# A CIN and DNN recommender kernel on one Trainium2 core: a rebuilt opening, in which TensorE turns the pair fields of the first two chunks

## The reference, cut to what matters

```
inputs = emb[feature_ids] * feature_vals[:, :, None]        # 1024 x 39 x 16
h = inputs
for i in range(3):                                          # sizes 200, 200, 200
    x = einsum('bhd,bmd->bhmd', h, inputs).reshape(B, -1, 16)
    x = relu(einsum('bcd,oc->bod', x, W[i]) + b[i])
    if i != 2: h, direct = x[:, :100], x[:, 100:]
    else: direct = x
    finals.append(direct)
d = relu(relu(inputs.reshape(B, -1) @ D0.T + d0) @ D1.T + d1)
out = concat(sum(finals over the 16), d) @ fc_W.T + fc_b + sum(bias_emb[ids] * vals)
```

## Time and profile before

| what | us |
|---|---|
| median of 3 runs | 2806.42 (2805.46 to 2812.66) |
| the profiled execution | 2815.94 |
| its span, first to last instruction | 2813.8 |
| PE busy in the span | 2652.6 (94%) |
| first matmul | 102.0 |
| PE without a gap from | 165.1 |

### The profile page before, as it was taken

The page is one execution under the profiler, slowest core; times in us unless marked ns, Lnnn a source line. Parts: engine busy times, 40 slices in busy tenths (PEclk is TensorE's granted clock), DMA queues, the critical chain, the costliest instruction groups (busy, mean ns, idle before and its releaser), DMA issues.

```text
span 2813.8 us, 66205 instructions
## 1 busy us (share of the span) xinstructions
PE 2652.6 (94%) x17912; PEld 2642.9 (94%) x17912; DVE 2269.9 (81%) x4563; ACT 1825.8 (65%) x4774; POOL 2256.7 (80%) x1921
## 2 busy tenths in 40 slices
PE   0279999999999999999999999999999999999998
PEld 0179999999999999999999999999999999999987
DVE  1278888888888888888887888888888888888873
ACT  0266767667666666666666767676766666666653
POOL 5388888888888888888888888888888888877753
PEclk9989999999999999999999999999999999999998
DMA  9734464444545464544554455545554546454531
GB/s 178 171 81 129 122 162 122 125 125 123 160 112 138 113 170 115 137 115 132 152 132 116 119 150 135 133 119 134 150 134 116 136 119 163 114 135 113 136 106 28
DMA packets 204534, 363.66 MB, mean 129 GB/s; under 512 B 66097, under 2 KB 118988, under 8 KB 204236
## 3 DMA queue, kind: packets, MB, share of 16 engines
q1 hardware_dynamic: 174080, 344.02, 44.7%
q0 software_dynamic: 10656, 2.92, 3.3%
q10 hardware_dynamic: 19628, 15.27, 2.0%
HBM read 357.87 MB, written 26.75 MB: 137 GB/s over the span
## 4 chain that ended last, share of the span: by engine, by line
PE 92%; ACTq 2%; POOL 1%; issue 1%; DMA 1%; SPq 1%; DVE 1%; ACT 0%; POOLq 0%; DVEq 0%
PE acc L564 60%; PE acc L565 28%; PE acc L586 2%; PE hrep L597 1%; ACTq L703 1%; DMA lin<-w 1%; POOL raw L441 1%; ACTq L682 0%; POOL xlo_p L487 0%; POOL prod_p L481 0%; DMA xs<-xt 0%; PE hrep L653 0%; SPq L295 0%; PE acc L632 0%; PE acc L631 0%
## 5 line engine op out<-in xcount | busy, mean ns | idle before, releaser
L564 PE MATMUL acc<-W,xhi_d 128*128 128x400 f32 x5632 | 1733.8, 367 | 15.7 <-DVE xlo_d L943 15.6
L565 PE MATMUL acc<-W,xlo_d 128*128 128x200 f32 x5632 | 1435.9, 255 | 0.0
L943 DVE TENSOR_TENSOR xlo_d<-prod_d,xhi_d 128x512 fp32r<-128x512 f32 (+1 forms) x1536 | 983.1, 640 | 220.2 <-ACT xhi_d L741 215.3
L935 DVE TENSOR_TENSOR prod_d<-hrep,xrep 128x512 f32<-128x512 f32 (+1 forms) x1536 | 1039.0, 677 | 100.5 <-ACT hrep L777 34.9
L487 POOL TENSOR_TENSOR xlo_p<-prod_p,xhi_p 128x512 fp32r<-128x512 f32 (+1 forms) x768 | 959.2, 1249 | 176.8 <-ACT xhi_p L735 128.4
L565 PEld LDWEIGHTS acc<-W,xlo_d 128*128 128x128 f32 x5632 | 1079.6, 192 | 0.0
L564 PEld LDWEIGHTS acc<-W,xhi_d 128*128 128x128 f32 x5632 | 1061.1, 188 | 17.4 <-DVE xlo_d L943 17.1
L564 PE MATMUL acc<-W,xhi_p 128*128 128x400 f32 x2944 | 917.8, 363 | 133.7 <-POOL xlo_p L487 133.7
L741 ACT ACTIVATE xhi_d<-prod_d 128x512 fp32r<-128x512 f32 (+1 forms) x1536 | 887.0, 578 | 236.4 <-PE acc L565 220.6
L481 POOL TENSOR_TENSOR prod_p<-hrep_s,xrep 128x512 f32<-128x512 f32 x512 | 667.4, 1304 | 163.7 <-ACT hrep_s L772 113.4
L565 PE MATMUL acc<-W,xlo_p 128*128 128x200 f32 x2944 | 751.8, 255 | 0.0
(11 more groups left out here) (79 smaller groups left out, 913.8 us busy)
## 6 DMA issues: line engine op xcount, KB each, us to landing
xrep<-xs SPq DMA_DIRECT2D x384, 384.0 KB, 4.3
l0x<-xs SPq DMA_DIRECT2D x384, 136.5 KB
xrep<-xs SPq DMA_DIRECT2D x384, 128.0 KB, 4.7
xrep<-xs SPq DMA_DIRECT2D x128, 336.0 KB, 5.1
xrep<-xe SPq DMA_DIRECT2D x128, 96.0 KB, 5.5
xe<-xs SPq DMA_DIRECT2D x40, 256.0 KB, 3.6
l0x<-xs SPq DMA_DIRECT2D x384, 19.5 KB
lin<-w ACTq DMA_DIRECT2D x8, 750.0 KB, 7.8
```

Source lines behind the costliest of these rows:

```text
L564: pe.matmul(bank[:, 0:2 * OUTS], hi, w, start=first, stop=last, skip_group_check=True)
L565: return pe.matmul(bank[:, 0:OUTS], lo, w[:, 0:OUTS], start=False, stop=last, skip_group_check=True)
L935: nc.vector.tensor_tensor(to, h, xrep[:, (par + layer - 1) % 2, a:a + count, :], ALU.mult).then_inc(s_prod_d, 1)
L943: op = nc.vector.tensor_tensor(xlo_d[:, slot, 0:split], bank[:, 0:split], xhi_d[:, slot, 0:split].bitcast(F32), ALU.subtract)
```

## The change

- Table rows: the ids of tile 0 alone are worked out first, straight into `idx`, so that the gathers wait neither for the values nor for a copy on POOL.
- W1: its rows and its load are issued by SP (at the start) and no longer by ACT; ACT issues W0's 9 DMAs, splits W0 and all of W1, and then issues W2's rows. SP issues the load of W2 after the blocks of chunk 1. Both loads have 13 DMAs where they had 17.
- DVE splits W0 and W1, and only then scales tile 0 (`first_scale`; POOL did it).
- Layer 0 of chunks 0 and 1 needs no DRAM: DVE lays the pair fields out by samples in `xrep` (`lay_out_pairs`), PE turns them (`first_inputs`, 8 transposes for a chunk), DVE copies them to `l0x` (`first_layer0`).
- DVE turns the first `EARLY` = 4 chunks by themselves, and SP stores those ahead; the 12 others are turned later and stored after W2's load.
- W2 is split inside step 1, a piece each after D3, D4, D5 and D6; PE waits for the pieces one by one (`W2_NEEDED`).
- `xe` is gone. Block 3 is loaded out of `xs` by four DMAs where it had two.
- In the loop, store and `dense_in` come one chunk later, and the gathers are dealt out anew: 9 in step 0 and 6 in step 1 (12 and 9 before).

```diff
-            def split_weights(layer):
+            def split_weights(layer, n):
...
+            dve.wait_ge(s_ids_in, 16)
+            table_rows(slice(0, FIELDS), idx[:], 0)
+            table_rows(slice(0, TILES * FIELDS), idi[:], 4)
...
-            split_weights(0)
-            turn_inputs(0, False)
+            split_weights(0, [0])
+            split_weights(1, range(len(PIECES[1])))
+            first_scale()
+            dve.wait_ge(s_xin, 2)
+            lay_out_pairs(0)
+            turn(0, EARLY, s_xt0)
+            lay_out_pairs(1)
+            first_layer0(0, (prod_d[0], prod_d[1]))
+            turn(EARLY, DIM, s_xt)
+            first_layer0(1, (prod_d[2], acc[2]))
             dve.wait_ge(s_fc, 32)
             evacuate(0, 0)
-            split_weights(1)
...
-            split_weights(2)
...
+            def first_inputs(c, banks):
+
+                pe.wait_ge(s_pairs, 2 * c + 2)
+                for n in range(L0_SLOTS):
+                    t = pe.transpose(banks[n // 4][0:L0_ROWS, n % 4 * P:(n % 4 + 1) * P], pairs(c)[:, n, :], ident[:])
+                    if n % 4 == 3:
+                        t.then_inc(s_pt, 1)
...
-            store_inputs(0)
-            sp.wait_ge(s_xs, 128)
-            load_layer0(0)
+            sp.wait_ge(s_xt0, 1)
+            store_rows(0, 0, EARLY, s_x0)
+            sp.wait_ge(s_x0, 128)
             sp.wait_ge(s_wlo, W_DONE[0])
-            for e in (1, 2, 0):
+            for e in (1, 2, 0, 3):
                 load_block(0, 0, e)
-            spread_inputs(0)
-            sp.wait_ge(s_prod_p, p_num(-1, 1) + 1)
-            load_layer0(1)
-            sp.wait_ge(s_one, 16)
-            sp.wait_ge(s_xe, 16 * XE_DMAS)
-            load_block(0, 0, 3)
-            for e in (1, 2, 0, 3):
-                sp.wait_ge(s_xblk[e], 32)
-                load_block(1, 1, e)
+            sp.wait_ge(s_pt, 4)
             sp.wait_ge(s_prod_p, p_num(0, 1) + 1)
             load_layer0(2)
+            for e in (1, 2, 0, 3):
+                sp.wait_ge(s_xblk[e], BLOCK_SEM[e])
+                load_block(1, 1, e)
+            load_weights(sp, 2, w2)
+            sp.wait_ge(s_xt, 1)
+            store_rows(0, EARLY, DIM - EARLY, s_xs)
+            store_dense_inputs(0)
             step(1, 0)
```

More of the change, by code:

```diff
@@ L81, in step_order @@
 def step_order(i):
-    return [g for g in ORDER if layer_of(*g) in present(i)]
+    order = [g for g in ORDER if layer_of(*g) in present(i)]
+    if isinstance(i, int) and i == 0:
+        order.sort(key=lambda g: layer_of(*g))
+    return order
 def p_num(i, k):
@@ new lines, in rows_of_weights @@
+        def rows_of_weights(engine, layer, src):
+            used = H_QUARTER * FIELDS
+            full = used // QUARTER
+            for q in range(4):
+                rows = lin[layer][used * q:used * (q + 1), :]
+                engine.dma_start(rows[0:full * QUARTER, :].rearrange("(t s) o -> s t o", s=QUARTER),
+                                 src[QUARTER * q:QUARTER * (q + 1), 0:full, :]).then_inc(s_lin[layer], 16)
+                engine.dma_start(rows[full * QUARTER:used, :],
+                                 src[QUARTER * q:QUARTER * q + used - full * QUARTER, full, :]).then_inc(
+                                     s_lin[layer], 16)
@@ L285, in _, with store_rows @@
             sp.wait_ge(s_pad, 1)
-            sp.dma_start(xe[:, QUARTER - 4:QUARTER, 4, :],
-                         prod_p[:, 2, :].rearrange("p (r n) -> p r n", n=P)).then_inc(s_one, 16)
+            load_weights(sp, 1, w1)
+            def store_rows(first, at, count, done):
+                for q in range(4):
+                    for j, n in ((0, QUARTER), (1, M_ALL - QUARTER)):
+                        sp.dma_start(
+                            xs[bass.ds(first + at, count), QUARTER * j:QUARTER * j + n,
+                               QUARTER * q:QUARTER * (q + 1)].rearrange("d c b -> c d b"),
+                            xt[QUARTER * q:QUARTER * q + n, at:at + count, j, :]).then_inc(done, 16)
             def store_inputs(tile):
@@ L466, in product @@
                 if k == 0:
-                    pool.wait_ge(s_l0x, (i + 2) * 96)
+                    if isinstance(i, int) and i < 1:
+                        pool.wait_ge(s_l0c, (i + 2) * 2)
+                    else:
+                        pool.wait_ge(s_l0x, i * 96)
                 elif k == 2:
@@ L503, in step @@
                     low(i, k)
-            FREE_AT = 7
+            FREE_AT = 8
+            COUNTS = [2] * 5 + [3] * 9 + [2]
+            BEFORE = sum(COUNTS[0:DIM - 1 - FREE_AT])
             def gathers(j):
-                for m in range(FIELDS):
-                    if m * (DIM - 1) // FIELDS == (j - FREE_AT - 1) % DIM:
+                n = (j - FREE_AT - 1) % DIM
+                if j != FREE_AT:
+                    for m in range(sum(COUNTS[0:n]), sum(COUNTS[0:n + 1])):
                         gather(m)
@@ L516, in _ @@
             pool.wait_ge(s_ids, 4)
-            copy_idx(0, 1)
             for m in range(FIELDS):
                 gather(m)
-            pool.wait_ge(s_pad, 1)
-            scale(0, False)
-            copy_idx(1, 2)
+            pool.wait_ge(s_ids, 8)
+            pool.wait_ge(s_gather, 16 * FIELDS)
+            copy_idx(1, 1)
+            pool.wait_ge(s_xin, 3)
+            gather(0)
             product(-1, 1, 0)
             step(-1, 1, 0)
-            pool.wait_ge(s_one, 16)
-            early = [m for m in range(FIELDS) if m * (DIM - 1) // FIELDS < DIM - 1 - FREE_AT]
-            step(0, 0, 0, early[0:12])
-            step(1, 1, 0, early[12:])
+            step(0, 0, 0, range(1, 10))
+            step(1, 1, 0, range(10, BEFORE))
             with pool.Fori(0, TILES - 1) as k:
@@ L889, in _ @@
             for buf in range(2):
-                nc.vector.memset(xrep[H_MAIN:P, buf, LAST_T, :], 1.0)
-            assert 2 * KT[0] * OUTS <= LAST_T * P
+                for t in (SPARE + 4, LAST_T):
+                    nc.vector.memset(xrep[H_MAIN:P, buf, t, :], 1.0)
+            assert 2 * KT[0] * OUTS <= (SPARE + 4) * P
             for l in range(2):
@@ new lines, in first_layer0, with split_weights @@
+            def first_layer0(c, banks):
+                if c > 0:
+                    dve.wait_ge(s_prod_p, 2 * c)
+                for n, bank in enumerate(banks):
+                    dve.wait_ge(s_pt, 2 * c + n + 1)
+                    nc.vector.tensor_copy(l0x[0:L0_ROWS, 4 * n:4 * n + 4, :].rearrange("p s n -> p (s n)"),
+                                          bank[0:L0_ROWS, :]).then_inc(s_l0c, 1)
+            def split_weights(layer, pieces):
+                for n in pieces:
+                    a, b = PIECES[layer][n]
@@ L972, in step @@
                     low(i, d)
+                    if isinstance(i, int) and i == 1 and d in W2_AT:
+                        split_weights(2, [W2_AT[d]])
                     if d == 3 and 1 in layers and not (isinstance(i, int) and i < 2):
```

208 lines of the change are left out of this document (112 added, 96 removed).

## The result

The changed kernel takes 2771.25 us (median of 4 runs, 2769.01 to 2776.8), the kernel before in the same job 2808.92 (4 runs, 2805.46 to 2812.66): ratio 0.9869, interval 0.9847 to 0.989, 37.7 us less (30.9 to 43.0). The forecast was 2760, 46.6 less than its median of the kernel before, 2806.42. The time lies in its range of 2742 to 2784, 11 us above its value; 2.5 of the 11 are the kernel before, whose median is 2808.92 here. The profiled execution is 2769.01.

What follows compares the result with a forecast made beforehand. The loop was taken to be at PE's floor, so only the opening could give time: D0 of step 1 55.6 us earlier, less 6 and 3, makes 46.6 off the median 2806.42, hence 2760, range 2742 to 2784.

Steps and rivals of the forecast that it cites:

- the slower rival: Loop: block 3 lands late in every step, so PE waits in each of 126 steps; 2836 us, chance 0.03.
- the forecast's own signs of being wrong: W1's last DMA past 65 or before 48, ACT waiting over 3 us for W2, or DVE waiting for `xrep` each step.
- W1 landed (ACT's split starts): Opening: with W0 and W1 on two queues, W1 lands at 57.5 us, between 51 and 61.
- POOL's first product: Opening: POOL begins chunk 0's product at 74.0 us against 98.31, 24.3 earlier.
- end of step -1 on POOL: Opening: POOL finishes both chunks' products and subtractions at 80.4 us against 114.34, 33.9 earlier.
- end of step 0 on POOL: Opening: step 0 keeps 20.5 of its 32.9 us and ends at 100.9, 46.3 earlier.
- D0 of step 1 on PE: Opening: with W2's split no longer ahead, D0 starts at 109.5 us against 165.08, 55.6 earlier.
- from there to the mark, more than the 32.5 of before: D0 to PE's first `hbuf` transpose in step 2: 6 us charged for DVE and POOL, 3 for SP's queue.
- lead at the mark: PE's first transpose of `hbuf` in step 2, behind all of the opening: 46.6 us earlier than before.
- the rival at 2750: Opening: two queues outrun the gathers, W1 is in at 51 and W2 earlier; 56 us gained, chance 0.20.
- The likeliest case: Whole kernel: the sum of the terms, 46.6 us earlier, gives 2760, own range 2752 to 2769, chance 0.51.
- the rival of SP's queue: Opening: W2's load, two stores and all blocks in order on SP's queue end it; 32 us gained, 2774, chance 0.24.

Runs made afterwards that it cites:

- again: The changed kernel measured once more with no edit: 2770.22 us, ratio 0.9858 to the kernel before.
- 13 gathers: Changed kernel with only 13 of the 39 gathers of tile 0, the other 26 fields left as zeros: 2762.99 us (one execution).
- W2 early: Changed kernel, W2's rows on SP behind W1, its first part loaded before the early store: 2771.51 us; also two gathers moved before step -1: 2769.06.
- the second pair: Second profiles of both kernels, neither edited: the kernel before at 2811.9 us, the changed kernel at 2770.22.

## Why the prediction came out as it did

The sign and the main mechanism were right: the opening gave nearly all of the time, DVE and SP were never late enough in the loop to stop PE, and block 3 (the slower rival) did no harm. The sum was 9.4 us too large for the opening, and one of the forecast's own signs of being wrong came: it allowed ACT 3 us of waiting for W2, and ACT waited 7.12. Its terms, measured at their ends:

| step | forecast | after | again |
|---|---|---|---|
| W1 landed (ACT's split starts) | 57.5 | 63.66 | 64.97 |
| POOL's first product | 74.0 | 78.64 | |
| end of step -1 on POOL | 80.4 | 84.49 | |
| end of step 0 on POOL | 100.9 | 104.88 | |
| D0 of step 1 on PE | 109.5 | 112.26 | |
| from there to the mark, more than the 32.5 of before | 9 | 15.7 | |
| lead at the mark | 46.6 | 37.2 | 36.2 |

*W1 lands: 6.2 us off.* This is the first step that failed. I took 57.5, between 51 (two queues outrun the gathers) and 61 (nothing changes), and both bounds were too low. All three rest on W1's data being there some 1 us behind its last issue, for which there was no row. In the kernel after the last issue ends at 58.51 (61.3 before) and W1 is there at 63.66, so about 4 of the 6.2 us are this landing, and only 2 are the issues. The DMA engines are nearly idle in it (40 slices of 57 to 66 us, in tenths):

```profile
DMA  9989844954231111201111111000000000029499
```

Nothing was gained by the second queue either: in the chain, W1's rows took 25.70 us to reach DRAM in the kernel after, and 16.48 in the kernel before:

```profile
13.25 25.70 DMA lin<-w
```

```profile
13.97 16.48 DMA lin<-w
```

(The first is the kernel after, the second the kernel before in its second execution.) W0's halves were summed at 42.34, for 43.28 before, so W1's 8.6 us (39.0 for 30.4) bought W0 nearly nothing. The queues show who has the DMA engines in 20 to 40 us (packets, MB, share), first in the kernel after, then in the kernel before:

```profile
q0 software_dynamic: 528, 0.14, 62.4%
q1 hardware_dynamic: 1378, 1.25, 19.8%
q10 hardware_dynamic: 1367, 1.04, 16.5%
```

```profile
q0 software_dynamic: 487, 0.13, 60.2%
q10 hardware_dynamic: 2985, 2.29, 36.8%
```

The two hardware queues together have 36.3% where one had 36.8%: they share what the gathers leave. The Trainium skill (DMA: Bandwidth & Descriptors, "Issuing engines are not separate DMA queues") says that a second issuer only saves the time to issue, and the run with W1 on ACT's queue agrees: 64.13 there, 63.66 and 64.97 on two queues. The rule by which two queues outrun the gathers (the rival at 2750) gave 51, and no run with all its gathers came near it.

*From W1 to POOL's first product: 1.5 us better.* 14.98 us where I had 16.5; the split took 9.0 for 9.95, and scaling, layout, eight transposes and the copy 6.0 for 6.5. Both terms were priced from rows and came out within 1 us. So did the 20.5 us of step 0 (20.4); its store took 4.5 and not 7.5.

*D0 of step 1:* 2.8 us late in all, W1's 6.2 less what the middle gave back.

*Step 1: 6.7 us off.* This is the second step that failed. I charged 6 for DVE and POOL and 3 for SP's queue, and it lost 15.7. PE waited 10.1 of them (5.6 in the stop behind ACT's 7.12 for W2), and its matmuls took the other 5.6 more than before, at the lower clock. The chain says what set the time: from 120.29, where W2 is there, it runs through ACT and DVE alone to PE's last wait, at 139.15. Up to that matmul PE is 13.3 us behind the kernel before (26.9 us from D0 for 13.6), from there to the mark 2.3 more. So most of the slow matmuls ran in time that PE would else have waited. Only the nine pairs behind 139.15 delayed the mark, 0.25 us each, and the kernel before has nine such pairs behind its own D0. The clock needs next to no term here (worked out from the rows, not tested by a run).

What was mis-sized are both charges. DVE stood idle 6.15 us for W2, where I had 3 for SP's queue: I had W2 landing at 108 to 112, "where ACT wants it at about 111", and it landed at 120.3, since its rows start when ACT has split W1, 6 us late, and its load issues at 96 and not at 90. And the split took DVE some 10.6 us in the step for 8.1, the rest being waits for POOL (the 128x2400 piece 4.66 us, the 64x200 one from `odd` 1.34 for 0.36), against which I had also set all of DVE's 2.8 us of slack. POOL's own longer rows, the reason that I gave beside DVE, made PE wait for nothing behind D0.

The likeliest case had an own range of 2752 to 2769, and the time lies 2 us above it, near the rival of SP's queue (2774). That rival's first condition, an early store of 12 us, did not come (4.5), and neither did its second, a wait of PE at step 2; what was late is W2's landing. Whether SP's queue or the DMA engines set that landing is open. The chain of the kernel after runs through SP's issues from 87.97 to 113.78 without a pause of more than 0.5 us, which speaks for the queue; SP's queue holds 94.1% of the engines from 96 to 120 us meanwhile, which speaks for the bytes; and with the largest piece of W2 on ACT's queue the mark stays. One figure is firm. From the start of W1's split to the mark the kernel after takes 96.7 us, its repeat 96.8, W1 on ACT's queue 96.8, 13 gathers 96.9, W2's main part on ACT's queue 97.0, W2 early 96.5 and 96.1, all chunks in one store 98.1. Only TensorE's turn (108.5 without it), the pieces of W2's split (100.9 in one) and the subtraction left out (94.0) move it. What sets this constant wasn't taken apart further: no run had less W2 to load.

*The end of the sum.* "The two short stops of PE may come or go" was too easy. They cost the kernel before 9.3 us and the kernel after 1.9 in these executions, and which of them stays depends on how the gathers are dealt out to steps, which the change did alter. By the marks the pair of profiles gives 37.2 in the opening, 7.4 in the loop and 2.0 at the end; the second pair 36.2, 4.2 and -1.8, 38.6 in all. The end of the program differs by some us between executions (2.0 and -1.8 in the two pairs). The medians' 37.7 (30.9 to 43.0) covers 38.6, and not quite 46.6.

## What to carry to other kernels

A load that is the opening's bound wasn't made faster by another issuing queue while gathers held the DMA engines; take bytes or passes off its path (TensorE turning 128x117 tiles in place of a trip through DRAM gave 12 us), or move the gathers. Give a landing a term of its own behind the last issue: here it was 5.2 us, nearly as much as the whole error of the step. Where PE waits for another engine and its clock is low as well, don't add the two up: follow the chain, and count only the slow matmuls behind the last wait. And if a short stop repeats at the same place in two executions, count instructions up to it before calling it chance.

## What the runs showed of the hardware that was not expected

- In all 14 profiles POOL stands 5.2 to 7.1 us ahead of its 114th and its 227th gather when the gather before it has only just ended, by count and not by time (590 to 608 us, 1542, 1754); with some 17 us of other work between the two gathers it stands 0.5 us. What POOL waits for is not shown; that the time between the two gathers covers it is.
- The 39 gathers of the first tile moved about 0.3 MB and held 54.8% of the DMA engines from 19 to 62 us in the kernel before, 43.7% in the kernel after. With 26 of them left out, the weight load beside them was there 10 us earlier.
- DVE and POOL hold each other up, in both directions, in DVE's subtractions of the weights. The Trainium skill (SBUF — State Buffer, "SBUF: two separate sides") has the shared port pair as an exclusive lock: a DVE instruction with two SBUF inputs and a GpSimd instruction that reads SBUF can't both have it, and the one that starts second blocks until the first is done. For POOL's gathers the trace agrees: those at 126.20 and 131.30 end 0.9 us, a gather's own time, behind DVE's ends at 127.74 and 133.66. For DVE it agrees too: the 8-column subtraction (the run without W2's low part) took 0.17 us alone and 1.89 beside POOL, and the 4.66 of the 128x2400 piece in the kernel after are 2.1 until POOL's subtraction ended at 131.13, and 2.5 of its own. But the 64x200 one at 134.10 in the run with 8 columns waited for two instructions of POOL that by the profile started after it, at 134.66 and 135.90, which the page doesn't have. The forecast let all six gathers of step 1 wait; two did, and a third took 1.42.
- The granted clock fell to 0.50 behind a stop of PE of 5.6 us and stayed there until about 144 us, through a stretch in which PE had four more stops of 0.3 to 1.7 us: 13 matmuls in 3 us where 23 fit. In the kernel before it was 0.50 behind a stop of 9.35 us, too, and back by about 170.3, 5 us on, PE having worked without a gap.
